# Reordered setup lists on five engines of an adaptive-norm mixer and expert kernel

## The reference

```python
mod = (silu(c) @ wmod).reshape(32, 6, 1, 256)      # sa, ca, ga, sb, cb, gb per row
ga, gb = sign * max(|.|, 0.25)
h = layernorm(x) * (1 + ca) + sa
S = scan over tokens: s = a*s + (1-a)*h            # a = sigmoid(decay_logit)
x = x + ga * (S @ W.T + b + conv5(h) + conv_b)
h = layernorm(x) * (1 + cb) + sb
e = argmax(gelu(h[last token] @ Wp1 + bp1) @ Wp2 + bp2)   # one of 8 experts per row
out = (gelu(h @ W1[e] + b1[e]) @ W2[e] + b2[e]) @ Wo + bo
x = x + gb * (h + 0.3 * out)
```

## Time and profile before

| | before |
|---|---|
| median of 3 runs | 674.09 us (673.1 to 675.87) |
| the profiled execution | 675.26 us, its span 673.1 us |
| TensorE busy | 644.6 us, 96% |
| VectorE busy | 558.7 us, 83% |
| ACT busy | 561.9 us, 83% |
| POOL busy | 444.9 us, 66% |
| DMA | 120.58 MB, mean 179 GB/s |

### The profile page before, as it was taken

The page is one execution under the profiler, slowest core; times in us unless marked ns, Lnnn a source line. Parts: engine busy times, 40 slices in busy tenths (PEclk is TensorE's granted clock), DMA queues, the critical chain, the costliest instruction groups (busy, mean ns, idle before and its releaser), DMA issues.

```text
span 673.1 us, 11162 instructions
## 1 busy us (share of the span) xinstructions
PE 644.6 (96%) x3469; PEld 532.9 (79%) x3469; DVE 558.7 (83%) x863; ACT 561.9 (83%) x976; POOL 444.9 (66%) x536
## 2 busy tenths in 40 slices
PE   2988999999999999999999999999999999999986
PEld 2976878888888888888888888888888888888765
DVE  1096888999999999999999999999999999998612
ACT  1477798889888889988889888889988889887753
POOL 1476467766767776667766667877667666676543
PEclk8599999999999999999999999999999999999999
DMA  9499764555556545455455565655545564555541
GB/s 306 166 284 339 211 195 147 174 168 185 162 184 189 187 142 214 127 166 172 153 187 187 159 188 189 188 165 148 166 163 175 157 187 171 176 157 156 156 157 63
DMA packets 55454, 120.58 MB, mean 179 GB/s; under 512 B 5643, under 2 KB 43364, under 8 KB 46180
## 3 DMA queue, kind: packets, MB, share of 16 engines
q1 hardware_dynamic: 51844, 115.65, 54.3%
q10 hardware_dynamic: 3552, 4.23, 2.2%
HBM read 61.12 MB, written 25.19 MB: 128 GB/s over the span
## 4 chain that ended last, share of the span: by engine, by line
PE 84%; DMA 8%; DVE 2%; ACT 1%; SPq 1%; issue 1%; POOL 1%; DVEq 0%; ACTq 0%
PE U L1047 10%; PE U L1049 8%; PE TR L1087 8%; PE U L1048 8%; PE Q L1067 8%; PE Q L1062 8%; PE Q L1063 8%; PE Q L1079 4%; DMA up_w<-up_table 4%; PE Y L1031 4%; PE Y L1027 4%; PE Y L1028 4%; PE TR L1079 4%; DMA xr<-in_L_ffn_W_dram 2%; PE Y L984 2%; PE U L1102 2%
## 5 line engine op out<-in xcount | busy, mean ns | idle before, releaser
L453 POOL TENSOR_TENSOR g_lo<-g,g_hi 128x512 fp32r<-128x512 f32 x128 | 170.3, 1333 | 148.7 <-ACT g_hi L613 146.5
L833 DVE SCALAR_TENSOR_TENSOR Y<-h,taps,Y 128x512 f32<-128x512 f32 x320 | 222.3, 749 | 2.6 <-PE Y L1031 0.3
L1047 PE MATMUL U<-hid_hi,up_w 128*128 128x512 f32 x256 | 110.1, 430 | 4.3 <-DMA up_w<-up_table 3.2
L1062 PE MATMUL Q<-g_hi,down_w 128*128 128x512 f32 x256 | 103.7, 405 | 0.3 <-issue 0.3
L565 ACT ACTIVATE S<-xr,nmr,rstd 128x256 f32<-128x256 f32 x128 | 66.6, 592 | 41.4 <-POOL S_lo L461 40.0
L1063 PE MATMUL Q<-g_hi,down_w 128*128 128x512 f32 x256 | 101.1, 395 | 0.0
L1049 PE MATMUL U<-hid_lo,up_w 128*128 128x512 f32 x256 | 100.8, 394 | 0.0
L1048 PE MATMUL U<-hid_hi,up_w 128*128 128x512 f32 x256 | 100.6, 393 | 0.0
L606 ACT ACTIVATE g<-U,up_w 128x512 f32<-128x512 f32 x128 | 87.2, 681 | 10.1 <-PE U L1049 9.9
L781 DVE BATCH_NORM_STATS2 st<-xr 128x6 f32<-128x512 f32 x128 | 88.0, 708 | 8.0 <-DMA xr<-in_L_attn_x_dram 3.7
L878 DVE TENSOR_TENSOR_SCAN S<-keep,h 128x512 f32<-128x512 f32 x64 | 75.6, 1218 | 21.0 <-ACT h L683 21.0
(11 more groups left out here) (116 smaller groups left out, 1283.5 us busy)
## 6 DMA issues: line engine op xcount, KB each, us to landing
up_w<-up_table SPq DMA_DIRECT2D x32, 1027.0 KB, 6.7
down_w<-down_tab SPq DMA_DIRECT2D x32, 1024.0 KB, 8.6
xr<-in_L_attn_x_dram SPq DMA_DIRECT2D x32, 512.0 KB, 3.6
out_dram<-xr SPq DMA_DIRECT2D x64, 256.0 KB, 2.3
xr<-in_L_ffn_W_dram ACTq DMA_DIRECT2D x5, 512.0 KB, 10.9
xr<-in_L_ffn_W_dram SPq DMA_DIRECT2D x4, 512.0 KB, 9.4
up_table<-g_lo SPq DMA_DIRECT2D x2, 1024.0 KB, 9.3
up_table<-down_w SPq DMA_DIRECT2D x2, 1024.0 KB, 11.4
```

Of the source, the lines that this page charges most:

```text
L453: nc.gpsimd.tensor_tensor(g_lo[:, f], g[:, f % 2], g_hi[:, f].bitcast(f32), ALU.subtract).then_inc(g_lo_ready, 1)
L833: ins = nc.vector.scalar_tensor_tensor(out=Y[c][:, :], in0=h[:, c, k:k + T], scalar=taps[:, c, k:k + 1], in1=Y[c][:, :], op0=ALU.mult, op1 ...
L1047: mm(U[f % 2][:, :], up_w[:, par, UP + w:UP + w + P], hid_hi[:, par, c], start=(c == 0), stop=False)
L1062: mm(Q[c][:, :], down_w[:, par, 1, w:w + P], g_hi[:, f], start=(f == 0), stop=False)
```

## The change

The setup lists of all five engines are in another order. No function is added, removed or altered, and the lists of the slots are as before. What moves:

- SP issues the vectors first, then x of row 0 and W2(0), the taps, and only behind the first two parts of wmod (`for_modulations`) W1(0), Wo, W2(1), W, x(1), W1(1). W1(2) goes behind the modulation. The splits 0, 1 and 2 go behind W1(5) and x(2); the router's weights go behind split 4, beta behind split 5.
- POOL: `w1_lo(2)` and `w1_lo(3)` ahead of `gates`, `norm1(2)` ahead of `s_low0(1)`, `hid_low(0)` ahead of `s_low0(2)`.
- ACT: `xn1_of(0)` first, W1's rounding (`w1_hi`) amid the copies of W2 and of the products with Wo.
- VectorE: `betas` and the second `down_low` earlier or later, `residual1(0, 0)` and `residual1(1, 0)` earlier, `s_low1(2)` last.
- TensorE: W's transposes and W2(1)'s ahead of row 0's `to_channels`; `mix(0)` behind `comb(1, 1)`, `mix(1)` behind `comb(4, 0)`; `back_to_tokens` later or earlier by one or two steps.

```diff
 SP
             def prologue():
+                vectors()
                 load_x(0)
+                load_w2(0)
                 load_taps()
+
+                for_modulations()
                 load_w1(0)
+                load_wo()
+                load_w2(1)
+                load_w()
                 load_x(1)
                 load_w1(1)
-                vectors()
-                load_router()
-                load_w1(2)
-                load_w2(0)
-                load_w2(1)
-                load_wo()
-                load_w()
 
                 sp.wait_ge(s_mod_mm, 1)
                 load_w2(2)
+                load_w1(2)
+                b1_out()
                 load_w1(3)
-                split_out(0)
 
                 sp.wait_ge(s_wT, 1)
                 load_w1(4)
-
-                for_modulations()
-                split_out(1)
-                b1_out()
                 load_w1(5)
-                load_w1(6)
-                beta_out()
-                split_out(2)
-                split_out(3)
 
                 sp.wait_ge(s_mod_mm, 1)
                 load_x(2)
-                split_out(4)
+                split_out(0)
+                split_out(1)
+                split_out(2)
+                load_w1(6)
+                split_out(3)
 
                 sp.wait_ge(s_w2T_mm, 4)
                 load_w1(7)
+                split_out(4)
+                load_router()
                 split_out(5)
+                beta_out()
                 split_out(6)
...
 POOL
                 w1_lo(1)
-                w1_lo(2)
                 norm1(1)
                 s_low0(0)
+                w1_lo(2)
+                w1_lo(3)
                 gates()
-                w1_lo(3)
                 w1_lo(4)
+                norm1(2)
                 s_low0(1)
                 w1_lo(5)
-                norm1(2)
+                norm2(0)
                 w1_lo(6)
-                norm2(0)
                 w1_lo(7)
+                hid_low(0)
                 s_low0(2)
                 norm1(3)
-                hid_low(0)
 ACT
             def prologue():
+                xn1_of(0)
                 w1_hi(0)
-                xn1_of(0)
+                w2T_copy(0)
                 w1_hi(1)
-                w2T_copy(0)
-                w1_hi(2)
+                mix_high()
+                h_of(0)
                 down_high(0, 0)
-                h_of(0)
-                down_high(0, 1)
-                mix_high()
                 w2T_copy(1)
                 s_high(0, 0)
+                down_high(0, 1)
+                w1_hi(2)
+                w1_hi(3)
                 s_high(0, 1)
                 down_high(1, 0)
-                w1_hi(3)
                 w2T_copy(2)
+                xn1_of(1)
                 down_high(1, 1)
-                xn1_of(1)
                 w1_hi(4)
+                w1_hi(5)
+                down_high(2, 0)
+                down_high(2, 1)
+                w2T_copy(3)
                 h_of(1)
-                down_high(2, 0)
                 gate1(0)
-                w1_hi(5)
+                down_high(3, 0)
                 s_high(1, 0)
-                w2T_copy(3)
-                down_high(2, 1)
                 s_high(1, 1)
                 w2T_copy(4)
-                down_high(3, 0)
-                down_high(3, 1)
                 w1_hi(6)
                 w2T_copy(5)
+                down_high(3, 1)
+                down_high(4, 0)
...
 VectorE
                 stats1(1)
                 scan(0, 0)
+                betas()
+                down_low(0, 0)
                 down_low(0, 1)
+                scan(0, 1)
                 mix_low()
-                scan(0, 1)
                 s_low1(0)
                 down_low(1, 0)
                 dve.wait_ge(s_taps, 16)
                 conv(0, 0, 6)
-                betas()
-                conv(0, 6, 10)
                 down_low(1, 1)
+                conv(0, 6, 9)
                 down_low(2, 0)
+                conv(0, 9, 10)
+                stats1(2)
+                down_low(2, 1)
                 scan(1, 0)
                 scan(1, 1)
-                down_low(2, 1)
-                stats1(2)
+                residual1(0, 0)
+                down_low(3, 0)
                 s_low1(1)
-                residual1(0, 0)
                 residual1(0, 1)
-                down_low(3, 0)
...
                 down_low(7, 0)
-                residual1(1, 1)
                 down_low(7, 1)
+                s_low1(2)
 TensorE
                 w2_transposes(0)
+                w_transposes()
+                w2_transposes(1)
                 to_channels(0, xn1, xn1_ready, t1_done)
                 comb(0, 0)
+                betas()
                 comb(0, 1)
-                w_transposes()
-                w2_transposes(1)
-                betas()
+                w2_transposes(2)
                 comb(1, 0)
-                w2_transposes(2)
+                comb(1, 1)
                 mix(0)
-                comb(1, 1)
                 comb(2, 0)
                 w2_transposes(3)
+                comb(2, 1)
 
                 pe.wait_ge(s_beta3, DC)
                 to_channels(1, xn1, xn1_ready, t1_done)
-                comb(2, 1)
-                back_to_tokens(0)
                 w2_transposes(4)
                 comb(3, 0)
+                back_to_tokens(0)
                 comb(3, 1)
                 w2_transposes(5)
+                comb(4, 0)
                 mix(1)
-                comb(4, 0)
                 comb(4, 1)
                 w2_transposes(6)
...
                 w2_transposes(7)
+                back_to_tokens(1)
+                router_nav(0)
                 comb(6, 0)
-                router_nav(0)
-                back_to_tokens(1)
                 comb(6, 1)
```

More of the change, by code:

```diff
@@ L686, in prologue @@
             def prologue():
+                xn1_of(0)
                 w1_hi(0)
-                xn1_of(0)
+                w2T_copy(0)
                 w1_hi(1)
-                w2T_copy(0)
-                w1_hi(2)
+                mix_high()
+                h_of(0)
                 down_high(0, 0)
-                h_of(0)
-                down_high(0, 1)
-                mix_high()
                 w2T_copy(1)
                 s_high(0, 0)
+                down_high(0, 1)
+                w1_hi(2)
+                w1_hi(3)
                 s_high(0, 1)
                 down_high(1, 0)
-                w1_hi(3)
                 w2T_copy(2)
+                xn1_of(1)
                 down_high(1, 1)
-                xn1_of(1)
                 w1_hi(4)
+                w1_hi(5)
+                down_high(2, 0)
+                down_high(2, 1)
+                w2T_copy(3)
                 h_of(1)
-                down_high(2, 0)
                 gate1(0)
-                w1_hi(5)
+                down_high(3, 0)
                 s_high(1, 0)
-                w2T_copy(3)
-                down_high(2, 1)
                 s_high(1, 1)
                 w2T_copy(4)
-                down_high(3, 0)
-                down_high(3, 1)
                 w1_hi(6)
                 w2T_copy(5)
+                down_high(3, 1)
+                down_high(4, 0)
                 xn1_of(2)
                 w1_hi(7)
-                down_high(4, 0)
                 xn2_of(0)
@@ L725, in prologue @@
                 down_high(5, 0)
+                hid_high(0)
                 h_of(2)
                 gate1(1)
-                down_high(5, 1)
                 w2T_copy(7)
                 s_high(2, 0)
+                down_high(5, 1)
+                s_high(2, 1)
+                down_high(6, 0)
                 nav_of(0)
-                down_high(6, 0)
-                s_high(2, 1)
                 down_high(6, 1)
-                hid_high(0)
                 down_high(7, 0)
@@ L884, in prologue @@
                 mods_setup()
-                down_low(0, 0)
                 stats1(1)
                 scan(0, 0)
+                betas()
+                down_low(0, 0)
                 down_low(0, 1)
+                scan(0, 1)
                 mix_low()
-                scan(0, 1)
                 s_low1(0)
@@ L894, in prologue @@
                 conv(0, 0, 6)
-                betas()
-                conv(0, 6, 10)
                 down_low(1, 1)
+                conv(0, 6, 9)
                 down_low(2, 0)
+                conv(0, 9, 10)
+                stats1(2)
+                down_low(2, 1)
                 scan(1, 0)
                 scan(1, 1)
-                down_low(2, 1)
-                stats1(2)
+                residual1(0, 0)
+                down_low(3, 0)
                 s_low1(1)
-                residual1(0, 0)
                 residual1(0, 1)
-                down_low(3, 0)
                 down_low(3, 1)
+                down_low(4, 0)
                 conv(1, 0, 6)
-                down_low(4, 0)
+                down_low(4, 1)
                 conv(1, 6, 10)
-                down_low(4, 1)
                 scan(2, 0)
```

(8 more changed lines are left out.)

## The result

| | before | after |
|---|---|---|
| median of 4 runs | 673.88 us | 663.96 us |
| ratio, 95% interval | | 0.985 (0.982 to 0.988) |
| the profiled execution, its span | 675.26, 673.1 us | 665.03, 663.0 us |
| first product of row 0 | 87.50 us | 76.44 us |
| end of the transfers of the setup | 78.0 us | 68.0 us |

The account below looks back on a forecast made before the run. Setup before row 0's first product is bound by transfers as much as products; rows stay. First product 9.7 us earlier, less 0.3 in row 0, gives 9.4: from 674.09 to 664.7 us, range 661.0 to 669.5.

Parts of the forecast that it names:

- Modulation, start and end: Setup products on TensorE: start at 7.4 us, begin at 2.4 GHz, end at 14.4, bounds 12.6 and 18; before, end 26.6.
- The hole: Setup transfers: the 7.8 us with nothing to move closes, as the engines have work until 18.1 us.
- mix(0): Setup, row 0: starts at 30.4 us against 39.30, 8.9 us earlier, with W1(1) landing at about 19.4.
- W2(6): Setup load TensorE waits for next: issued by ACT at 45.3 us, 13.3 on its way, there at 58.6.
- From W2(6) to the choice: Setup tail, from W2(6)'s transposes to the choice of row 0's expert: 12.3 us, choice at 70.9.
- Choice to fetch: End of setup: fetch of the expert's weights issued 1.1 us behind the choice, at 72.0, landing 5.4 us later.
- rival 1: Transfers alone bind: W2(6) lands early or later data moves at 337 GB/s; gain 11 to 13.5, 661 to 663 us; chance 0.17.
- mix(2) and row 0: mix(2) waits for s_low1(2), first product at 77.8 us instead of 87.50; later conv(2) costs row 0 0.3 us.
- Rival 2: TensorE's clock falls in a new gap of over 5 us ahead of W2(6): 667 to 669.5 us; chance 0.21.
- Rival 3: TensorE's clock stays at 1.2 GHz behind the modulation, first product near 115 us: some 700 us; chance 0.05.
- The prediction's other reading: Transposes don't count for the clock, which waits for comb(0, 0): mix(0) at 31.3 us, the sum 0.9 us less.
- Rival 4: No effect: an issue the lists don't advance, such as a split behind POOL, ends the setup: 671 to 676 us; chance 0.05.

Follow-up runs that it names:

- dense_warm_up: The changed kernel with two float32 products of 512 columns in place of the 14 warm-up transposes: 663.1 us, ratio 0.983.
- hid_high_later: The changed kernel with hid_high(0) on ACT moved from ahead of h_of(2) to behind s_high(2, 1): 663.48 us, ratio 0.983.
- tail_both: The changed kernel with s_low1(2) moved behind down_low(6, 1) and hid_high(0) behind s_high(2, 1): 664.00 us, ratio 0.983.
- no_hold_for_wmod: The changed kernel without for_modulations() in SP's list, its wait for the first parts of wmod: 662.9 us, ratio 0.983.
- vec_late_again: The changed kernel with vectors() moved back behind load_w1(1) in SP's list: 679.1 us, ratio 1.006.
- other_lists_only: SP's list of the kernel before with the other four engines' lists of the changed kernel: 680.4 us, ratio 1.008.
- dense_and_hid_high: The changed kernel with two float32 products as warm-up and hid_high(0) moved behind s_high(2, 1): 663.28 us, ratio 0.984.
- sp_list_only: SP's list of the changed kernel with the other four engines' lists of the kernel before: 666.2 us, ratio 0.988.
- s_low1_earlier: The changed kernel with s_low1(2) moved from the end of VectorE's setup list to behind down_low(6, 1): 665.41 us, ratio 0.986.

## Why the prediction was right

The mechanism and the place held: a hole behind late vectors, closed, the rows unchanged. The sum came out near the time partly by luck. Three of its terms were wrong. The end of the modulation cost little. W2(6)'s way was put 3.3 us too long and the tail behind it 2.4 us too short, and these cancelled in part: the first product came 1.4 us earlier than forecast (76.44, not 77.8), of which row 24 took 0.6 back.

- *Modulation, start and end.* Start 7.4 forecast, 6.75 measured. End 14.4 forecast, 17.13 measured: the forecast let the clock start at 2.4 GHz. What failed is the reading of the granted clock in the earlier trace rows. It is recorded as 1.00 in the first 10 us of before (5 to 10 us below), but the warm-up transposes in the earlier trace rows took 3.25 us for 14, 0.23 each, where eight at the high level take 1.04, 0.13 each (at 21.41 us in the profile after). TensorE was slow while the column said 1.00. In the profile after, the column says 1.00 throughout, and both the modulation and W2(0)'s transposes (1.95 us for 8) are slow. In these traces the duration tells the level; the column agrees with it only once a fall has been recorded. The bound of 18 held.

```profile
5.00:10.00 5.00, 2.12 (x10) 1.72 (x9) 1.50 (x4) 0.83 (x3) 1.70 (x4) 1.00 0.98 357
```

- *The hole.* Closed, as forecast, and with a slack that took up the 2.7 us: the engines had work until 18 us.
- *mix(0)* at 30.4, measured 30.77. W1(1) landed at 10.65 + 8.7 = 19.35, forecast 19.4, but it did not bind here. ACT waited 2.22 us for W2(0)'s transposes, which the late modulation held back, and `w1_hi(1)` followed its copies without a wait at 19.89 us (lines below). With the modulation over early, W1(1) binds at 19.52 (dense_warm_up). The two conditions lie 0.4 us apart at this point, and that is why the wrong end of the modulation did little harm there.

```profile
18.93 0.59 ACT L579 COPY g<-U 128x512 f32<-128x512 f32 x1 [2.22 <-PE U L962]
...
19.89 1.06 ACT L573 CAST hid_lo<-hid 128x1024 fp32r<-128x1024 f32 x1
```

- *W2(6)*, issue at 45.3, measured 44.91. The way was 13.3 in the sum, 10.0 measured (7.5 to 10.7 in the eight other profiles of this order with early vectors). In both kernels W2(6) moved no data in its first 3 us, while SP's queue was full. After that its queue moved 0.09 MB a us before the change, beside 0.20 to 0.35 on SP's (60 to 64 us), and 0.17 and 0.29 after it, beside 0.06 (51 to 53 us). SP had issued no split between 40.57 and 49.51 us: split 5 went out as POOL's `w1_lo(5)` ended. "A split gated late would shorten the way", as the forecast said. No run moved the splits alone, so this cause fits but is not shown. The Trainium skill (DMA: Bandwidth & Descriptors, section Queues, rings and completion order) has engines take turns between queues packet by packet, which would give such a shorter way once no long packets stand beside it; the way here agrees in direction, 10.0 against 13.3.
- *From W2(6) to the choice*, 12.3 in the sum, 14.67 measured. The step counted TensorE's products alone. ACT's list, full from 56.6 to 65.7 us, is what it follows: 1.4 us idle before back_to_tokens(1), of them 1.23 for gate1(1), and 0.4 in the comb behind. The router's steps took 0.4 more than counted. hid_high_later took 0.86 us off it.
- *Choice to fetch* 1.1 forecast, 1.08 measured. The last split landed at 66.6, so the transfers did not bind; they ended 10.0 us earlier, not 7.8, since they moved at 334 instead of 311 GB/s. Both conditions of rival 1 were thus met, and the first product's 11.06 us are the low end of its gain. But transfers did not bind at the end, as the choice came later than the splits, and the time stayed outside its 661 to 663 us.
- *mix(2) and row 0.* The wait for s_low1(2) was 0.87 us, first product at 76.44 instead of 77.8, and 0.37 us given back in row 0 (0.3).

Rival 2, the clock falling in a gap ahead of W2(6): the gap was 0.85 us, and the comb behind it ran at 1.73 us as in the earlier trace rows. Rival 3: in the profile after, the transposes at 20.14 us still took 1.43 for eight and those at 21.41 took 1.04, so the level rose at some 21 us, 4 us behind the modulation, and in tail_both, the latest of the kernels with all five new lists and early vectors, the granted clock rose at some 23.6 us. The prediction's other reading, in which the clock waits for comb(0, 0), did not come true. Here the level rose among transposes, ahead of comb(0, 0) at 22.28 us. In dense_warm_up and no_hold_for_wmod the granted clock rose at 17.7 and 19.3 us, among transposes too, with comb(0, 0) at 19.98 and 20.56. Rival 4 is excluded by the interval.

## What to carry to other kernels

When a queue of transfers is full for most of a stage, look for the stretch in which it is empty and follow its cause back to one small transfer: here 28.5 KB behind 2 MB cost some 7 us, and moving them alone brought three quarters of the gain. Lists on engines that wait for each other are one piece of work: four of the five new lists without the fifth were 5.3 us slower than the old. A sum over the engine that seems to bind is not the path; the tail here followed ACT's list. And read the level of the clock from how long a known instruction takes before building on the recorded clock.

## What the runs showed of the hardware

- The level of TensorE's clock at the start differs from one execution to the next. Of 12 experiment profiles, five ran the modulation at 0.11 us a record from 7.6 us or earlier and fell to 0.216 between 9 and 11 us, seven had it at 0.216 throughout. Two of the seven (vec_late_again, other_lists_only) begin it only at 20.4 and 14.6 us, behind 12.9 and 7.1 us of idle TensorE. Of the ten that begin it by 7.3 us, it is five against five. Kernels with one and the same list up to there, and the same warm-up, stand on both sides (tail_both and hid_high_later; dense_warm_up and dense_and_hid_high). What decides it is open. What it is worth at mix(0) depends on when the level rises again: in dense_warm_up and no_hold_for_wmod it rose by 19.3 us and mix(0) came at 29.56 and 29.75; in tail_both it rose at 23.6 and mix(0) came at 31.19, no earlier than in the six slow profiles of the changed order (30.66 to 31.43).
- In all five the level fell while TensorE was working at the modulation, near the time, 10.8 us, at which it fell before the change with TensorE idle. In two (sp_list_only, dense_warm_up) it rose within the first products of the modulation. Rival 2 had counted the fall from the start of the idle stretch; these runs speak against that.
- Rows take 18.39 us each, but rows 8 and 24 took up to 19.54 and 19.82 us (s_low1_earlier), in some profiles and not in others, and rows 2 and 23 up to 19.1 in one profile each. In row 24 of the changed kernel TensorE waits for the weights of the next expert (the line below). These rows account for 0 to 2.6 us and, but for hid_high_later, for most of the spread behind the first product; why it is these rows is open.

```profile
537.92 0.50 PE L1048 MATMUL U<-hid_hi,up_w 128*128 128x512 f32 x1 [0.72 <-DMA up_w<-up_table]
```
